# Two small DMA jobs of a graph-attention kernel's edge stages moved from SyncE's queue to ScalarE's

## The reference

```python
h = (x @ W.T).reshape(n, 8, 32)
alpha = einsum('ehd,hd->eh', h[src], a_src) + einsum('ehd,hd->eh', h[dst], a_dst)
enc = relu(edge_attr @ edge_W.T + edge_b).reshape(-1, 8, 32)
alpha = leaky(alpha + sum(enc * h[dst], axis=-1))
ex = exp(alpha - segment_max(alpha, dst)[dst])
out = segment_sum(h[src] * (ex / segment_sum(ex, dst)[dst])[..., None], dst)
```

## Time and profile before

| what | value |
|---|---|
| time, 3 runs | 7784.48, 7785.42, 7786.51 us (median 7785.42) |
| the profiled execution | span 7807.0 us, 99204 instructions |
| busy share PE / DVE / ACT / POOL | 67% / 42% / 18% / 46% |
| first edge stage | about 240 to 3180 us, with 403 slots' loads |
| second edge stage | about 4495 to 7085 us, with 403 slots' loads |
| DMA | 1022 MB, mean 131 GB/s |

### The profile page before, as it was taken

The page is one execution under the profiler, slowest core; times in us unless marked ns, Lnnn a source line. Parts: engine busy times, 40 slices in busy tenths (PEclk is TensorE's granted clock), DMA queues, the critical chain, the costliest instruction groups (busy, mean ns, idle before and its releaser), DMA issues. The chain is left out here.

```text
span 7807.0 us, 99204 instructions
## 1 busy us (share of the span) xinstructions
PE 5257.7 (67%) x19729; PEld 3739.4 (48%) x19729; DVE 3278.9 (42%) x5938; ACT 1371.0 (18%) x2977; POOL 3613.4 (46%) x3708
## 2 busy tenths in 40 slices
PE   2387887788788878228999625556565556663498
PEld 1144444444444444227999514444444444442498
DVE  6255555555555555721111313333333333336244
ACT  2122222222222222002222200000000000000122
POOL 2635555555555554042222056666666666650222
PEclk9689999999999999658999857777777777786699
DMA  6434444444444443515666544444444444434255
GB/s 220 136 101 122 122 119 123 124 124 125 122 123 121 122 124 102 186 60 165 183 183 183 153 102 114 113 115 115 114 112 113 113 114 116 113 102 154 101 198 188
DMA packets 718013, 1022.24 MB, mean 131 GB/s; under 512 B 301733, under 2 KB 531561, under 8 KB 692608
## 3 DMA queue, kind: packets, MB, share of 16 engines
q0 software_dynamic: 183456, 485.95, 23.8%
q1 hardware_dynamic: 527676, 519.31, 21.7%
q10 hardware_dynamic: 6564, 14.14, 0.5%
HBM read 868.26 MB, written 153.27 MB: 131 GB/s over the span
## 5 line engine op out<-in xcount | busy, mean ns | idle before, releaser
L773 POOL DMA_INDIRECT e_rows<-sc_table,e_eidx x3224 | 3115.9, 966 | 2253.8 <-issue 952.6
L880 PE MATMUL e_ps_o<-e_rows,e_oh 128*128 128x264 f32 x6448 | 1918.5, 449 | 856.9 <-ACT e_res L969 700.8
L880 PEld LDWEIGHTS e_ps_o<-e_rows,e_oh 128*128 128x128 f32 x6448 | 1379.2, 222 | 1384.3 <-issue 1147.6
L1064 DVE SCALAR_TENSOR_TENSOR e_u<-e_encr,e_adst,e_ps_hd 128x512 f32<-128x512 f32 x806 | 597.1, 745 | 1160.2 <-remote 366.1
L1132 DVE TENSOR_TENSOR e_rows<-e_rows,e_ps_w 128x1024 f32<-128x1024 f32 x806 | 970.7, 1207 | 106.3 <-issue 83.5
L822 PE MATMUL e_ps_X<-e_u,e_hwide 128*104 128x512 f32 x1612 | 871.1, 635 | 16.8 <-DVE e_u L1064 14.8
L1055 DVE TENSOR_SCALAR e_ohT<-e_at,e_nid 96x512 bf16<-96x512 int16 x806 | 292.5, 363 | 1384.6 <-DMA e_aw<-sc_a2p 553.7
L969 ACT COPY e_res<-e_ps_o 32x264 f32<-32x264 f32 x806 | 296.0, 367 | 3291.4 <-PE e_ps_o L884 1242.4
L810 PE MATMUL e_ps_enc<-e_at,e_w_enc 96*128 96x512 bf16 x806 | 317.9, 394 | 570.6 <-ACT e_encr L942 383.4
L1676 PE MATMUL x_ps_h<-x_xT,x_w 128*128 128x256 f32 x2624 | 648.2, 405 | 15.4 <-DMA x_b<-in_L_ffn_b_dram 15.4
L1676 PEld LDWEIGHTS x_ps_h<-x_xT,x_w 128*128 128x128 f32 x2624 | 638.5, 337 | 20.6 <-issue 16.4
(11 more groups left out here) (290 smaller groups left out, 3538.7 us busy)
## 6 DMA issues: line engine op xcount, KB each, us to landing
x_w<-in_L_ffn_W_dram SPq DMA_DIRECT2D x112, 1024.0 KB
e_at<-sc_grp SPq DMA_DIRECT2D x403, 192.0 KB
x_w<-in_L_ffn_w_dram SPq DMA_DIRECT2D x60, 1024.0 KB
e_rows<-sc_table,e_eidx POOLq DMA_INDIRECT x3224
e_at<-sc_grp SPq DMA_DIRECT2D x403, 96.0 KB
sc_agg<-e_res SPq DMA_DIRECT2D x816, 33.0 KB
sc_xb<-r_zero SPq DMA_DIRECT2D x24, 1032.0 KB
x_xin<-sc_xb SPq DMA_DIRECT2D x86, 258.0 KB
```

The lines of the kernel that those rows point to most:

```text
L773: pool.indirect_dma_start(rows[:, k, s, j, :], None, dr["table"][:, :], bass.IndirectOffsetOnAxis(eidx[:, k, s, j:j + 1], 0)).then_inc(s_r ...
L880: nc.tensor.matmul(ps_o[:, 0:ROW], oh[:, k, at_j:at_j + P], rows[:, k, s, j, :], start=(j == 0), stop=False)
L1064: nc.vector.scalar_tensor_tensor(u[:, p, h, :], encr[:, h, :], adst[:, h:h + 1], ps_hd[:, h, :], ALU.add, ALU.mult).then_inc(s_u, 1)
```

## The change

- First edge stage: ACT issues the stores of the sums, two slots behind its own eviction (LAG = 2), between `evict` and the relus. For each it waits for the landing of the store before, and reads one word of `tab` into a register. ACT's eviction no longer waits for `s_out` there. SP keeps the loads, the tables and the flags.
- Second edge stage: ACT issues the two loads of a slot, right after each `evict`, four slots ahead of their use (LEAD = 4). There are 13 places instead of 5 (one for each slot of a block). SP keeps the stores, now of the slot just evicted, the tables and the flags. Before the loops ACT issues the first 13 loads at once and 17 more between its own steps.
- `blk` has two words for each slot instead of three; the 31 extra entries, three DMAs of the planning stage and one memset are gone, and SP's 31 stores after the loops become 26 (second stage) or none (first stage).

```diff
-BEHIND = 31
...
-        N_STORES = 8 + 2 + 2 + GT + GT + 2 * ST + 6
+        N_STORES = 8 + 2 + GT + GT + 2 * ST + 5
...
-                sp.dma_start(dr["blk"][0:TL, 0:2].rearrange("(t p) c -> p t c", p=P), blki[:, :, :]).then_inc(s_st, 16)
-                sp.dma_start(dr["blk"][BEHIND:BEHIND + TL, 2:3].rearrange("(t p) c -> p t c", p=P), blki[:, :, 1:2]).then_inc(s_st, 16)
+                sp.dma_start(dr["blk"].rearrange("(t p) c -> p t c", p=P), blki[:, :, :]).then_inc(s_st, 16)
...
-                act.dma_start(dr["blk"][0:BEHIND, 2:3].rearrange("r c -> c r"), npad[0:1, :]).then_inc(s_st, 16)
-                act.dma_start(dr["blk"][TL:TL + BEHIND, 0:2], zero[0:BEHIND, 0:2].bitcast(I32)).then_inc(s_st, 16)
...
+        PLACES = RING if first else SB
...
+        LAG, LEAD = 2, 4
...
+        def store(eng, t, s, passed):
+            if not isinstance(t, int) or t > 0:
+                hold(eng, s_out, t * 16 + OUT0, passed)
+            hold(eng, s_ev, t + (1 + EV0), passed)
+            n = first_node(eng, t)
+            eng.dma_start(dr["agg"][bass.ds(n, WIN), :], res[0:WIN, kept(s), :]).then_inc(s_out, 16)
...
             def phase(b, k):
                 for s in range(SB):
-                    t = b * SB + (2 * SB + s)
-                    hold(sp, s_hd if first else s_xa, t * PER - (behind(s) - 1) * PER, s_ps)
-                    g, n, back = entry(t)
-                    load(ring(s), g, n)
-                    store(t, s, back)
+                    t = b * SB + s
+                    if first:
+                        ahead = t + 2 * SB
+                        hold(sp, s_hd, ahead * PER - (behind(s) - 1) * PER, s_ps)
+                        g, n = group_and_node(sp, ahead)
+                        load(sp, ring(s), g, n)
+                    else:
+                        store(sp, t, s, s_ps)
...
             def evict(b, s):
                 t = b * SB + s
                 hold(act, s_o, t + (1 + O0), s_pa)
-                if not isinstance(t, int) or t + BEHIND - 2 * SB + 1 >= since(s):
-                    hold(act, s_out, t * 16 + 16 * (BEHIND - 2 * SB + 2 - since(s)), s_pa)
+                if not first and (not isinstance(t, int) or t >= since(s)):
+                    hold(act, s_out, t * 16 + (16 + OUT0 - 16 * since(s)), s_pa)
                 nc.scalar.copy(res[0:WIN, kept(s), :], ps_o[0:WIN, 0:ROW]).then_inc(s_ev, 1)
 
-            def phase(b, k, pre, turn, turns):
+            def store_behind(b, s):
+                t = b * SB + s - LAG
+                if not isinstance(t, int) or t >= 0:
+                    store(act, t, (s - LAG) % SB, s_pa)
+
+            def load_ahead(b, s):
+                t = b * SB + (2 * SB + s + LEAD)
+                hold(act, s_xa, t - (SB - 1), s_pa)
+                g, n = group_and_node(act, t)
+                load(act, ring((s + LEAD) % SB), g, n)
+
+            def phase(b, k, pre, turn, turns, ahead):
                 m, n = b + 1, b + 2
                 for s in range(SB):
                     evict(b, s)
+                    if first:
+                        store_behind(b, s)
+                    elif ahead:
+                        load_ahead(b, s)
                     if first and pre:
                         relu(n, s)
```

More of the change, by code:

```diff
@@ L620, in edge_phase @@
         s_nb, s_const, s_w, s_wp, s_we, s_init, s_ready = (sem(n) for n in ("nb", "const", "w", "wp", "we", "init", "ready"))
-        s_ld = [sem(f"ld{r}") for r in range(RING)]
+        s_ld = [sem(f"ld{r}") for r in range(PLACES)]
         s_ei, s_ns, s_fr, s_rows = ([sem(f"{n}{k}") for k in range(2)] for n in ("ei", "ns", "fr", "rows"))
@@ L635, in ring @@
         def ring(s):
-            return s % 4 if s < 12 else 4
+            return s if not first else s % 4 if s < 12 else 4
         def loads_of(b, s):
-            return b * (3 * N_LD) + (s // 4 + 1) * N_LD if s < 12 else b * N_LD + N_LD
+            return b * (3 * N_LD) + (s // 4 + 1) * N_LD if first and s < 12 else b * N_LD + N_LD
         def kept(s):
@@ L664, in _ @@
                 sp.dma_start(w_st[3:4, :], io["L0_gnn_edge_b"].rearrange("(a o) -> a o", a=1)).then_inc(s_w, 16)
[L666 to L670, removed]
             def tables(t, k):
@@ L681, in flags @@
                              ).then_inc(s_fr[k], 16)
[L683 to L697, removed]
             sp.wait_ge(s_ready, 1)
@@ L703, in _ @@
             sp.wait_ge(s_nb, 32)
[L704 to L708, removed]
-                load(ring(s), g, n)
[L710 to L719, removed]
+            if first:
+                for t in range(2 * SB):
+                    s = t % SB
+                    if t >= behind(s):
+                        sp.wait_ge(s_hd, (t - behind(s) + 1) * PER)
+                    g, n = group_and_node(sp, t)
+                    load(sp, ring(s), g, n)
+                    if t == 3:
+                        sp.wait_ge(s_wp, 1)
+                        for k in range(3):
+                            for i in range(3):
+                                sp.dma_start(w_enc[12 * k + 4 * i:12 * k + 4 * i + 4, :], w_part[:, k, :]).then_inc(s_we, 16)
+                    if t == SB + 6:
+                        sp.wait_ge(s_lk, 1)
+                        sp.wait_ge(s_dn, 2)
+                        tables(2 * SB, 0)
+            else:
+                sp.sem_inc(s_out, OUT0)
+                sp.wait_ge(s_lk, 1)
+                sp.wait_ge(s_dn, 2)
+                tables(2 * SB, 0)
             steps = steps_of(sp)
@@ L740, in _ @@
                     phase(i * 2 + (1 + q), 1 - q)
[L741 to L745, removed]
+            if not first:
+                for j in range(2 * SB):
+                    store(sp, steps * (2 * SB) + (SB + j), j % SB, s_ps)
+                hold(sp, s_out, steps * (32 * SB) + (48 * SB + OUT0), s_ps)
             hold(sp, s_ei[1], steps * 16 + 32, s_ps)
@@ L987, in _ @@
             if first:
+                act.sem_inc(s_out, OUT0)
                 for s in range(SB):
                     relu(0, s)
+            else:
+                act.wait_ge(s_nb, 32)
+                for t in range(SB):
+                    g, n = group_and_node(act, t)
+                    load(act, ring(t), g, n)
             sources(0, 0, 0)
```

66 lines of the change are left out of this document (48 added, 18 removed).

## The result

The changed kernel takes 7877.41 us in the median of four runs (7865.15 to 7882.78), the kernel before 7784.95 us (7766.66 to 7786.51) beside it: a ratio of 1.0122, with an interval of 1.0106 to 1.0139. It is 92 us slower; the forecast had 78. The profiled execution of the changed kernel has a span of 7871.4 us, 64 us over that of the profiled one before, so some 28 of the 92 us don't show in this pair of traces.

A forecast was written before the change was run, and what follows sets the result against it. A slot lasts for the longer of PE's round with ACT and POOL's four gathers with a tail. Terms 100 + 30 - 30 - 20 - 2 = +78 us on the median of 7785 gave 7863 us; overall range 7400 to 8450.

The forecast's parts named there:

- the likeliest case: Whole kernel: the forecast itself, 7863 us, own range 7740 to 8250, from a wholly hidden store to three quarters of 584; 34%.
- Stores in the first stage, +100: First edge stage: ACT's store ahead of the relus lengthens PE's round from 5.06 to 6.51 us; +100 us, bounds 0 and +584.
- The sixth of 1.45 us: First edge stage: share of ACT's added store step taken as exposed, 0.25 us a slot over 403 slots.
- if nothing hides it: First edge stage: upper bound of the store term, the whole step exposed, 403 x 1.45 = +584 us.
- a tail: Edge stages: PE's note coming late after POOL's four gathers, 1.05 us after their end, expected to hide part of ACT's step.
- `sources` behind the loads, +30: Second edge stage, slot 1 of each block: loads delay `sources`; 31 x 1.9 = 59 us bare, half covered, +30 us.
- Store landings, -30: Second edge stage: SP's stores go out and land earlier, shortening ACT's evict waits; -30 us, ends 0 and -356.
- Start of the second stage, -20: Second edge stage's start: first block's loads no longer take SP 127 us against POOL's 65; a third of 62 us, -20.
- Planning, -2: Planning stage: the second table DMA and two small ones go; -2 us, between 0 and -5.
- The jam gets lighter: Rival, both edge stages: fewer SP queue writes and late loads free half of PE's held-back notes; about 7450 us, 32%.
- Nothing shows: Rival, whole kernel: the tail covers the stores whole, the rest is -22 to 0; about 7770 us, 14%.
- ACT is slowed like SP: Rival, both edge stages: ACT issuing DMAs under gathers falls into SP's slow pace, delaying relus and evicts; about 8400 us, 20%.

The follow-up runs named there:

- e1: Kernel before with only the first stage's half: ACT issues the stores of sums, two slots behind the eviction; 7777.8 us, ratio 1.0073 to before.
- e2: Kernel before with only the second stage's half: ACT issues the loads into 13 places, SP the stores; 7763.9 us, ratio 1.0062 to before.
- e8: The changed kernel again, unaltered, measured beside other follow-up runs; 7815.9 us, ratio 1.0126 to before.
- e5: Changed kernel with ACT's store (first stage) and loads (second stage) as its last step of each slot; 7716.8 us, ratio 0.9999 to before.
- e6: Kernel before with one idle copy on ACT between evict and relus in every first-stage slot; 7779.8 us, ratio 1.0080 to before.
- e12: e10 run again where PE's notes come late; 7802.8 us, ratio 1.0000 to before.
- e3: Changed kernel with ACT's first-stage store behind the slot's two relus instead of ahead of them; 7785.7 us, ratio 1.0082 to before.
- series 3: Third set of runs on one chip, without late notes: e10, the kernel before and another variant; kernel before 6676.2 us as a follow-up run.
- series 2: Second set of runs on one chip, with late notes: e5, e6, e8 and a two-idle-copy variant; kernel before 7720 us.
- e10: e5 with the second block's loads, at the second stage's start, placed between leak, fade, power and place; 6616.7 us, ratio 0.9911 to before.

## Why the prediction was right, step by step

It was right in the sign and, at 78 against 92 us, nearly in the size, but not term by term. The parts were 60 us in the first stage and 43 in the second (e1, e2), and with 96 us for the whole (e8) some -7 are left for the rest; the forecast had 100, 0 and -22. So the nearness of the sum is in part luck: the store was priced 40 us too high, and two gains, -30 and -20, that hardly came made up for it.

Of the signs that were named, the relu 1.7 us after the eviction came (1.68), and so did POOL's longer waits for PE ahead of its gathers (from 495.0 to 642.2 us between 700 and 2900 us) and a second stage at 6.05 us a slot; the first stage's slot took 6.89 us, not 7.1. The ends of the likeliest case don't follow from the terms either: with a hidden store they give 7763 us, with three quarters of 584 they give 8201, not 7740 and 8250.

*Stores in the first stage, +100: the mechanism right, the size 60.* The relu follows 1.7 us after the eviction, as said; an idle copy of the same length costs the same. The sixth of 1.45 us was too much on both counts: ACT's step is 1.06 us (its register load 284 ns), and 0.15 us of it show. Of the 60, 37 are the relus; 33 more came back when the store also stood behind `sources` and the block's other steps, a second victim that the forecast named for the second stage alone. Over 31 blocks that is 1.07 us a block, just one store's step, but no run moved the store of slot 1 alone. That makes 70, and e5's stage came out 10 under before's, little more than the scatter of 7. The forecast didn't have the dropped wait ahead of the eviction, worth 0.15 us where notes are on time; that it gave the 10 us is not shown. The bound "if nothing hides it" was nearly met as well: 398 us in the series without a tail, against 403 x 1.45 = 584, or 427 at the 1.06 us that the step took.

*`sources` behind the loads, +30: right in kind, 43 in the controlled runs.* Its trace is PE's wait for `sources`, not DVE's for the leak, which stays in e5. The term took 59 us bare, at 1.9 us a load, and halved it for stuck notes. The step is 1.58 us and 49 us bare, and 43 of them showed: the price was too high, and the cover that was to halve it hardly there.

*Store landings, -30: wrong, it is 0.* e5 keeps SP's early stores and has the length of before's second stage, though the evictions' waits that the view puts down to a landing are down to 115.9 us from the 237.6 of e6, which has the old stage. So such waits were worth nothing by themselves.

*Start of the second stage, -20: most of it given back.* Two rows of before, and then the same two of after with the second block's first load:

```profile
4562.45 0.54 ACT L946 COPY e_alog<-e_rows 128x416 f32<-128x416 f32 x1 [90.39 <-DMA e_rows<-sc_table,e_eidx]
4594.69 0.60 ACT L950 ACTIVATE e_y<-e_ps_X 104x512 f32<-104x512 f32 x1 [31.70 <-issue]
```

```profile
4619.96 0.54 ACT L957 COPY e_alog<-e_rows 128x416 f32<-128x416 f32 x1 [89.59 <-DMA e_rows<-sc_table,e_eidx]
4622.78 0.60 ACT L961 ACTIVATE e_y<-e_ps_X 104x512 f32<-104x512 f32 x1 [2.28 <-issue]
...
4650.96 0.51 ACT L973 COPY e_rows<-e_ps_w 128x416 f32<-128x416 f32 x1 [7.61 <-remote]
4651.65 0.32 ACTq L665 DMA_DIRECT2D e_at<-sc_grp  x1
```

The leak came 32.2 us after `sources` and now comes 2.8 us after it: the first block's loads are in time, 29 us are won. But the second block's loads stand behind place in ACT's program and begin only at 4651.65, so the first sum comes hardly sooner: 164.3 us after the first gather, before 169.8. Of the 20 us 5.5 came. Moving those loads forward (e12) gave nothing more.

*Planning, -2: about right.* The first eviction came 6.2 us earlier in this pair. Over all runs with late notes it starts at 464.4 us in the mean with the new table (462.2 to 466.5, five traces) and at 467.8 with the old one (466.4 to 469.6, six): 3.3 us.

*The rivals.* "The jam gets lighter" fell by its own sign: in the second stage, from 4700 to 6900 us, the eviction starts 2.19 us after the sum's last matmul in the mean before and 2.07 us after it now, and e8 and e6, with the new stage and the old, both have 2.10. A fall of 0.3 us or more was asked for. "Nothing shows" fell with the relus. What spoke for it was the Trainium skill (DMA: Bandwidth & Descriptors, "Issuing engines are not separate DMA queues"): issuing on another engine saves only the time that it takes to issue. No view used here times a load's landing, so no run here shows whether that holds. "ACT is slowed like SP" was a true mechanism that didn't decide. It is in the changed kernel itself: at the start of the second stage its loads begin 4671.85 - 4662.02 = 9.8 us apart. In the first stage no store was slowed there. The argument that ACT issues right after POOL has begun fits, but it isn't shown: with the store as last step (e5) none took over 387 ns to issue either, while behind the relus (e3) one took 1122 ns.

## What to carry to other kernels

A step that is moved to another engine costs by what stands behind it in that engine's order, not by its length alone: the same store and loads cost 99 us as the first thing of a slot and nothing as the last. So give an engine its new step behind everything that another engine waits for, once-a-block steps included. And price a delay against the slack that it eats: here the first microsecond cost 0.15 us a slot, the second 0.65, and where the slack was missing the first cost 0.99.

## What the runs showed that was not expected

- The late notes are not a property of the kernel alone. In series 3 the same kernel before ran in 6678 us instead of the 7719 to 7802 of the others, with PE's notes to ACT in 0.27 us and SP's loads at 317 to 365 ns, under the same gathers. The cause stays open. It need not be the chip: the record has number 3 for the chip of series 2, with late notes, and of series 3, without them. It changes what an edit is worth: the first stage's half of the change costs 0.8% with late notes and 6% without.
- The slowing under gathers takes ACT too, once it issues in the middle of unbroken gathers: 9.2 us for a load's two DMAs and what goes with them, against 1.5 us (e12), and 9.8 us in the changed kernel.
- The version with store and loads last (e10) is 0.9% faster than the kernel before where notes are on time (0.9911 [0.9895, 0.9926]) and equal where they are late (1.0000 [0.9990, 1.0010]); it never ran in one series with the changed kernel, but e5, which differs from it at the start of the second stage alone, is 1.3% faster than the changed kernel (7716.8 against 7815.9 us).
